# Attention loop of a transformer block: transposes moved in TensorE's order, scores in two PSUM banks

## What is computed

```python
q = (h @ Wq_c @ Wq_up).reshape(b, t, H, D).transpose(0, 2, 1, 3)         # 16 heads of 128
q = rmsnorm(apply_partial_rope(q, cos, sin), q_norm_w)
k_sw = rmsnorm(apply_partial_rope(h @ Wk, cos, sin), k_norm_w)
v_sw = h @ Wv
ck = rmsnorm(h.reshape(b, nb, M * HID) @ W_comp, k_norm_w)               # one key for 16 tokens
c_scores = jnp.einsum('bhtd,bnd->bhtn', q, ck) * scale
c_out = attend(c_scores, valid[None, None], sink, ck, 'bhtn,bnd->bhtd')
sw_scores = CAP * jnp.tanh(jnp.einsum('bhtd,bsd->bhts', q, k_sw) * scale / CAP)
sw_out = attend(sw_scores, sw_mask[None, None], sink, v_sw, 'bhts,bsd->bhtd')   # window of 128
ao = (c_out + sw_out).transpose(0, 2, 1, 3).reshape(b, t, G, H // G * D)
inter = jnp.einsum('btgf,gfi->btgi', ao, Wg)
return inter.reshape(b, t, G * INTER) @ Wo
```

## Time and profile before

| what | us |
|---|---|
| median of 3 runs | 987.6 |
| lowest, highest run | 986.24, 991.37 |
| the profiled execution | 990.28 |
| its span | 988.5 |
| PE busy in the span | 907.0 (92%) |
| DVE, ACT, POOL busy | 664.4, 570.2, 561.8 |

### The profile page before, as it was taken

The page is one execution under the profiler, slowest core; times in us unless marked ns, Lnnn a source line. Parts: engine busy times, 40 slices in busy tenths (PEclk is TensorE's granted clock), DMA queues, the critical chain, the costliest instruction groups (busy, mean ns, idle before and its releaser), DMA issues. The chain is left out here.

```text
span 988.5 us, 16804 instructions
## 1 busy us (share of the span) xinstructions
PE 907.0 (92%) x5022; PEld 771.4 (78%) x5022; DVE 664.4 (67%) x1256; ACT 570.2 (58%) x1565; POOL 561.8 (57%) x759
## 2 busy tenths in 40 slices
PE   4988898789999999999899999999859899999996
PEld 4987685578888888887788888888748688888885
DVE  4464559588888888889988888888846433332312
ACT  0544454577777777777777777777444523324221
POOL 0155100578898888888888889888323323222222
PEclk9998989999999999999999999999979999999999
DMA  8556667213224133141241331422071020020101
GB/s 284 186 203 235 212 217 227 89 43 126 68 71 146 43 117 111 52 144 48 78 140 55 119 96 51 152 87 82 12 266 75 1 85 1 1 86 1 43 0 44
DMA packets 68725, 101.29 MB, mean 102 GB/s; under 512 B 16176, under 2 KB 48432, under 8 KB 65712
## 3 DMA queue, kind: packets, MB, share of 16 engines
q1 hardware_dynamic: 56528, 72.65, 23.1%
q10 hardware_dynamic: 12128, 27.71, 7.8%
HBM read 82.64 MB, written 26.35 MB: 110 GB/s over the span
## 5 line engine op out<-in xcount | busy, mean ns | idle before, releaser
L1054 PE MATMUL banks<-fold,aoT 128*128 128x512 f32 x768 | 193.1, 400 | 0.0
L1854 POOL TENSOR_TENSOR gus<-arena,gus 128x512 fp32r<-128x512 f32 x43 | 64.8, 1507 | 183.2 <-ACT gus L1756 183.2
L1054 PEld LDWEIGHTS banks<-fold,aoT 128*128 128x128 f32 x768 | 139.5, 188 | 27.8
L1820 DVE SCALAR_TENSOR_TENSOR arena<-banks,sg,arena 128x512 f32<-128x512 f32 x44 | 33.0, 751 | 133.0 <-ACT arena L1751 133.0
L1054 PE MATMUL banks<-k_st,qT 128*128 128x256 f32 x768 | 106.9, 288 | 0.0
L1751 ACT ACTIVATE arena<-banks,sg 128x512 f32<-128x512 f32 x44 | 30.2, 687 | 124.7 <-PE banks L1710 124.7
L1710 PE MATMUL banks<-hT_even,w_hi 128*128 128x512 f32 x352 | 86.6, 398 | 12.5 <-issue 9.7
L1054 PEld LDWEIGHTS banks<-k_st,qT 128*128 128x128 f32 x768 | 95.3, 189 | 0.5 <-DVE qT L1323 0.5
L1674 PE MATMUL banks<-w_hi,gus 128*128 128x512 f32 x352 | 87.2, 390 | 1.9 <-DVE gus L1825 1.1
L1710 PEld LDWEIGHTS banks<-hT_even,w_hi 128*128 128x128 f32 x352 | 66.1, 191 | 27.9 <-issue 10.1
L1431 POOL TENSOR_TENSOR pp<-pp,kons 64x512 fp32r<-64x512 f32 x64 | 84.2, 1316 | 4.1 <-ACT pp L1194 4.1
(11 more groups left out here) (198 smaller groups left out, 2153.8 us busy)
## 6 DMA issues: line engine op xcount, KB each, us to landing
arena<-in_wq_blocks ACTq DMA_DIRECT2D x8, 1056.0 KB, 4.8
wq_words<-in_wq_blocks ACTq DMA_DIRECT2D x8, 1056.0 KB, 6.9
w_lo<-wq_words SPq DMA_DIRECT2D x11, 768.0 KB, 9.2
go_raw<-in_w_go SPq DMA_DIRECT2D x16, 512.0 KB, 6.8
k_st<-k_parts SPq DMA_DIRECT2D x32, 192.0 KB, 2.8
arena<-in_L_attn_h SPq DMA_DIRECT2D x32, 128.0 KB, 3.4
comp_raw<-in_w_comp SPq DMA_DIRECT2D x16, 256.0 KB, 4.0
v_st<-v_parts SPq DMA_DIRECT2D x32, 128.0 KB, 2.1
```

The lines of the kernel that those rows point to most:

```text
L1054: last = pe.matmul(out, lhs[a], rhs[b], start=start and q == 0 and u == 0, stop=stop and q == n - 1 and u == 2)
L1820: dve.scalar_tensor_tensor(gu[:, n % 2], GU[2 * (n % 2) + 1][:], sg[:, 1, h:h + 1], gu[:, n % 2], ALU.mult, ALU.mult).then_inc(gued, 1)
L1854: pool.tensor_tensor(gus[:, n % 2, 1], gu[:, n % 2], gus[:, n % 2, 0].bitcast(F32), ALU.subtract).then_inc(gu_lo, 1)
```

## The change

PE's order within a step is changed. The transposed queries stand directly behind the scores, and the compressed transposes stand between the two halves of the projection. The three kinds of transposes have a bank each: compressed in bank 2, probabilities in bank 3, queries in bank 5 as before. The scores of four heads, 256 columns each, go to banks 0 and 1, two heads in a bank. The waits on PE follow the banks. The leftover products use banks 2, 3, 6 and 7. On POOL `rotate` is written as two operations, one behind the other. The orders of ACT, DVE, POOL and SP stay. The diff, cut to its core (what is left out replaces `T` by `T_PROBS` or `T_COMP` in the evictions, and moves the helper `over` out of `rotate`):

```diff
--- before.py
+++ after.py
@@ -226,8 +226,8 @@
-UNIT_BANK = (0, 1, 6, 7)
-UNIT_FREE = (5, 6, 11, 12)
+UNIT_BANK = (2, 3, 6, 7)
+UNIT_FREE = (7, 8, 11, 12)
...
@@ -974,7 +974,8 @@
     Q, T, O, Y = bank[4:8]
-    S = banks[:, 0:4]
+    T_COMP, T_PROBS = bank[2:4]
+    S = banks[:, 0:2].rearrange("p b (u n) -> p (b u) n", n=KEYS)
...
@@ -1071,7 +1072,6 @@
         def transpose_query(g):
             wait(pe, "q_rope", g.n())
-            wait(pe, "cT_lo", g.n(2))
             wait(pe, "qT_lo", g.n(1))
...
             if opening(g, 0):
-                pe.wait_ge(units.f_lo, H - HG + 2)
+                pe.wait_ge(units.f_lo, HG + 2)
...
@@ -1097,21 +1097,20 @@
         def transpose_probs(g):
             wait(pe, "p_nrm", g.n())
             wait(pe, "p_nrm3", g.n())
+            wait(pe, "p_lo", g.n(1))
+            if opening(g, 0):
+                pe.wait_ge(units.f_lo, H - HG + 2)
+            for h in range(HG):
+                last = pe.transpose(T_PROBS[:, h * P:(h + 1) * P], prob[:, g.j, h, 0:P], ident)
+            last.then_inc(s["pT_mm"], 1)
+
+        def transpose_compressed(g):
+
+            wait(pe, "c_nrm", g.n())
             wait(pe, "cT_lo", g.n(1))
-            ahead = At(g.m, g.c + 1, 0)
-            if ahead.live:
-                wait(pe, "qT_lo", ahead.n())
-            for h in range(HG):
-                last = pe.transpose(T[:, h * P:(h + 1) * P], prob[:, g.j, h, 0:P], ident)
-            last.then_inc(s["pT_mm"], 1)
-
-        def transpose_compressed(g):
-
-            wait(pe, "c_nrm", g.n())
-            wait(pe, "p_lo", g.n())
             for pair in range(2):
                 cols = slice(pair * P, (pair + 1) * P)
-                last = pe.transpose(T[:, cols], pc[:, g.slot, cols], ident)
+                last = pe.transpose(T_COMP[:, cols], pc[:, g.slot, cols], ident)
             last.then_inc(s["cT_mm"], 1)
...
-        steps(pe, (0, query), (3, transpose_probs), (2, scores), (3, transpose_compressed), (4, project_first),
-              (4, project_second), (1, transpose_query), (3, window_values), (3, compressed_values), alone=EVERY,
+        steps(pe, (0, query), (3, transpose_probs), (2, scores), (1, transpose_query), (4, project_first),
+              (3, transpose_compressed), (4, project_second), (3, window_values), (3, compressed_values), alone=EVERY,
...
-            act.activation(pp[:, g.slot, HIGH], T[:], ACT.Copy).then_inc(s["p_hi"], 1)
+            act.activation(pp[:, g.slot, HIGH], T_PROBS[:], ACT.Copy).then_inc(s["p_hi"], 1)
...
         def rotate(g):
...
+        def rotate_rest(g):
+            x = qn[:, g.slot]
             wait(pool, "q_r1", g.n(1, 3) + 2)
...
         steps(pool, (3, masked_high), (0, square_sum), (0, rsqrt), (2, compressed_less_max), (5, add_tile),
-              (2, over_sum_last), (0, rotate), (2, compressed_over_sum), after={1: first_deviation})
+              (2, over_sum_last), (0, rotate), (0, rotate_rest), (2, compressed_over_sum), after={1: first_deviation})
```

More of the change, by code:

```diff
@@ L1110, in transpose_compressed @@
             wait(pe, "c_nrm", g.n())
-            wait(pe, "p_lo", g.n())
+            wait(pe, "cT_lo", g.n(1))
             for pair in range(2):
                 cols = slice(pair * P, (pair + 1) * P)
-                last = pe.transpose(T[:, cols], pc[:, g.slot, cols], ident)
+                last = pe.transpose(T_COMP[:, cols], pc[:, g.slot, cols], ident)
             last.then_inc(s["cT_mm"], 1)
@@ L1200, in compressed_high @@
                 rows = slice(half * NB, (half + 1) * NB)
-                last = act.activation(pcS[rows, g.slot, :, half], T[rows, 0:2 * P].rearrange("p (a n) -> p a n", n=P), ACT.Copy)
+                last = act.activation(pcS[rows, g.slot, :, half], T_COMP[rows, 0:2 * P].rearrange("p (a n) -> p a n", n=P), ACT.Copy)
             last.then_inc(s["cT_hi"], 1)
@@ L1303, in probs_low @@
             wait(dve, "p_hi", g.n())
[L1304 removed]
+            dve.tensor_tensor(pp[:, g.slot, LOW], T_PROBS[:], pp[:, g.slot, HIGH].bitcast(F32), ALU.subtract
                               ).then_inc(s["p_lo"], 1)
@@ L1310, in compressed_low @@
                 rows, across = slice(half * NB, (half + 1) * NB), slice((1 - half) * NB, (2 - half) * NB)
-                last = dve.tensor_tensor(pcS[across, g.slot, :, half], T[rows, 0:2 * P].rearrange("p (a n) -> p a n", n=P),
+                last = dve.tensor_tensor(pcS[across, g.slot, :, half], T_COMP[rows, 0:2 * P].rearrange("p (a n) -> p a n", n=P),
                                          pcS[rows, g.slot, :, half].bitcast(F32), ALU.subtract)
@@ L1449, in compressed_less_max, with over @@
                                ALU.subtract).then_inc(s["c_sub"], 1)
+        def over(g, lo, n):
+            return rope_st[:, g.tile_slot, lo:lo + n].unsqueeze(1).broadcast_to([P, HG, n])
         def rotate(g):
@@ L1454, in rotate @@
             wait(pool, f"rope_in{g.tile_slot}", g.loaded())
-            over = lambda lo, n: rope_st[:, g.tile_slot, lo:lo + n].unsqueeze(1).broadcast_to([P, HG, n])
             x = qn[:, g.slot]
-            pool.tensor_tensor(ropb[:, :, 0:HALF], x[:, :, HALF:2 * HALF], over(2 * HALF, HALF),
+            pool.tensor_tensor(ropb[:, :, 0:HALF], x[:, :, HALF:2 * HALF], over(g, 2 * HALF, HALF),
                                ALU.mult).then_inc(s["q_r1"], 1)
-            pool.tensor_tensor(ropb[:, :, HALF:], x[:, :, 0:HALF], over(3 * HALF, HALF), ALU.mult).then_inc(s["q_r1"], 1)
+            pool.tensor_tensor(ropb[:, :, HALF:], x[:, :, 0:HALF], over(g, 3 * HALF, HALF), ALU.mult).then_inc(s["q_r1"], 1)
+        def rotate_rest(g):
+            x = qn[:, g.slot]
             wait(pool, "q_r1", g.n(1, 3) + 2)
-            pool.tensor_tensor(x[:, :, 0:2 * HALF], x[:, :, 0:2 * HALF], over(0, 2 * HALF), ALU.mult).then_inc(s["q_r1"], 1)
+            pool.tensor_tensor(x[:, :, 0:2 * HALF], x[:, :, 0:2 * HALF], over(g, 0, 2 * HALF), ALU.mult).then_inc(s["q_r1"], 1)
             wait(pool, "q_r1", g.n(per=3))
```

1 line of the change is left out of this document (removed).

## The result

The changed kernel takes 1043.4 us (median of 4 runs, 1040.7 to 1049.0) against 986.9 for the kernel before (the 3 runs above and one more). The ratio is 1.057, with a 95% interval of 1.052 to 1.062: slower by 56.5 us. The forecast was 1046.4 us, 1030 to 1064, and slower with 0.92.

What follows compares the result with a forecast made beforehand. It took a loop over PE, ACT and DVE to bound the changed kernel: intervals of 60.4, 120.0 and 356.8 us made 537.2 against 480.4, +56.8, with the end +58.8, on the median of 987.6 giving 1046.4 us, range 1030 to 1064.

Steps and rivals of the forecast that it cites:

- The bound and the spare: Loop from query over compressed transposes, ACT and DVE to next query: 7.14 us before, under PE's 7.89, 0.75 to spare.
- the part on the banks: Shared score banks and separate transpose banks: gain nearly zero, since PE lost next to nothing there; at most 0.1 us a step.
- The ordinary steps: Forty intervals of the attention loop, set by the PE, ACT and DVE loop at 4.58 + 4.34 = 8.92 us each.
- The steps behind `add_tile`: Thirteen intervals with `add_tile` in POOL's row; the loop through POOL's rotation to the query transposes sets 9.23 us each.
- The steps at the start of a batch: Six intervals with two masking instructions between `compressed_max` and `window_sum` on DVE; 10.07 us each.
- the rival of the clock: PE's idling lowers its clock to 0.85 in the loop, adding 0.8 us in 59 intervals: 1094 us; chance 0.04.
- The end: After the last query: three steps about 1 us late each, against half a projection before PE's 3.19 us wait; +2 us, 0 to +4.
- The early query transposes: Query transposes behind the scores need `q_rope` early; ordinary loop through POOL 8.63 us, hidden under 8.92.
- ACT's own loop: From `compressed_high` through `over_sum` and PE back to the compressed transposes: 8.26 to 9.25 us, taken as 8.5, hidden under 8.92.
- PE as the bound: Rival: PE keeps 7.89 us a step and loses its 7.1 + 5.8 us of waits, about 975 us; chance 0.06.
- The loops of POOL and ACT alone: Rival: only these loops bind, ordinary steps 8.6 us, first of a batch 9.8, 1032 us in all; chance 0.12.
- The signs: Expected profile: steps about 8.9 us, PE idle 0.9 to 1.1 ahead of queries, ACT waiting at `compressed_high`, clock at 1.00.

Runs made afterwards that it cites:

- e9_add_tile_behind: The changed kernel with POOL's `add_tile` moved behind the rotation and `compressed_over_sum`; 1035.7 us, ratio 1.049 to the kernel before.
- e6_dve_only: The changed kernel with `compressed_low` moved behind `window_sum` and `scale_query` on DVE, ACT's order left; 1124.4 us, ratio 1.141 to the kernel before.
- e1_banks_only: The changed kernel with PE's order of before, keeping the new banks and waits; 981.9 us, ratio 0.995 to the kernel before.
- e3_compressed_late: The changed kernel with the query transposes back behind the projection, compressed transposes still between its halves; 1014.4 us, ratio 1.028 to the kernel before.
- e4_both_evictions_behind: The changed kernel with `compressed_high` behind tanh and exp on ACT, `compressed_low` behind `window_sum` and `scale_query` on DVE; 977.0 us, ratio 0.988 to the kernel before.
- e8_split_three: The changed kernel with three heads of the projection ahead of the compressed transposes and one behind, for two and two; 1101.7 us, ratio 1.118 to the kernel before.

## Why the prediction was right

**The bound and the spare.** The reasoning from the earlier trace rows held: from compressed transposes to query 4.34 us were read and 4.27 measured. One statement beside it was wrong: "nothing in it waits" did not hold for the step of the earlier trace rows: 0.25 us ahead of the compressed transposes were a wait, and PE's floor is 7.63 us. Without that wait the loop of the kernel before was 2.55 + 4.27 = 6.82 us, which is 0.81 under the floor, where I had 0.75. It changed no conclusion, but it is the term that was mis-sized. For the same reason the part on the banks was not quite right: "PE lost next to nothing there" leaves out these 0.25 us a step.

**The ordinary steps.** 8.92 us forecast, 8.74 measured, 40 of them: 7 us less. Query to compressed transposes is 0.77 + 0.35 + 1.51 + 0.35 + 1.48 = 4.46, not 4.58: the 1.51 stands against the 1.75 that held the wait, and in part made up for it are a longer query (0.77 for 0.69) and half projection (1.48 for 1.42). The way back is 4.27 for 4.34, most of it 0.41 for 0.47 from PE to ACT.

**The steps behind `add_tile`.** 9.23 forecast, 9.21 to 9.40 measured, 120.9 us in thirteen for 120.0; e9_add_tile_behind shows the cause.

**The steps at the start of a batch.** 10.07 forecast. Three of the six took 9.95 to 9.97 us, three 11.47 to 11.52. The difference is the clock. Two steps in a row and an ordinary one (stretch, length, busy us and instructions of PE, PEld, DVE, ACT and POOL, granted clock, DMA):

```profile
484.75:496.22 11.47, 9.03 (x46) 7.67 (x47) 8.40 (x18) 6.56 (x22) 7.97 (x12) 0.86 0.00 0
496.22:506.17 9.95, 7.54 (x46) 6.38 (x47) 8.32 (x17) 6.56 (x22) 7.00 (x11) 1.00 0.34 99
...
295.87:304.60 8.73, 7.88 (x49) 6.74 (x50) 7.13 (x15) 6.45 (x22) 6.82 (x11) 1.00 0.26 76
```

In the step from 484.75 the granted clock was 0.86 on average, that is, PE ran at the 1.2 GHz level for a part of it: its three query matmuls took 1.62 us for 0.93. PE had idled 2.42 us ahead of them. The next one had 2.44 us ahead of it and stayed at 1.00. Where the idle was 0.85 us a step, the clock stayed at 1.00 throughout. So the rival of the clock, to which I gave 0.04 for the whole loop, was true of three steps and cost 4.6 us. The Trainium skill (TensorE: Matmul & The Clock Gate, A second HAM failure mode: psum-queue depth-cycling) tells of a kernel in which short idles made the clock swing. The rows agree in part for idles of 2.0 to 2.5 us in a step of ten (three of seven here, about one in five in e6_dve_only), and do not for 0.85 us in 8.7.

The three parts give 349.7 + 120.9 + 64.4 = 535.0 us against the 537.2 of the sum: 7.1 us too much for the ordinary steps, 0.9 and 4.0 too little for the other two. That the sum was nearer than its terms is luck.

**The end.** +2 us estimated, 0 to 4; measured +4.8, outside of that. The lateness of the three steps came as forecast, 0.8, 1.0 and 1.0 us (728.01, 737.09, 746.04, 753.92 from step to step, for 682.01, 690.32, 698.29, 705.21 before). But I had set half a projection against PE's wait of 3.19 us. That wait only changed its name (PE, last query and the projection in that step):

```profile
728.01 0.93 PE L1055 MATMUL banks<-wup,q_st 128*128 128x512 f32 x3 [0.86 <-DVE qn L1331]
...
757.07 2.45 PE L1055 MATMUL banks<-fold,aoT 128*128 128x512 f32 x6 [2.50 <-DVE aoT L1277]
```

`project_first` needs `aoT`, whose low part stands on DVE behind the statistics for the next stage. PE waits 2.50 us for it, and the six matmuls then take 2.45 us instead of 1.64, at a granted clock of 0.62. The step that failed is that the wait "now has half a projection, 1.42 us, before it": DVE's queue held that half too.

**The other edits.** Banks: nothing forecast; in e1_banks_only the median is 5.7 us lower, the loop 1.8. The early query transposes: free, as said. ACT's own loop was hidden: PE waited for `over_sum` three times, all behind the last query.

**The rivals.** PE as the bound was out by 68 us. The loops of POOL and ACT alone, 8.6 us a step, would have come near the 8.74, but it is DVE's `qn` in front of the query that PE waits for in every ordinary step, and POOL's `qn` only 12 times; and with the query transposes late again (e3_compressed_late) half the loss stays. The Trainium skill (Perfetto Trace Analysis, Identifying the Most-Contended Engine) would have had the engine with the highest occupancy optimised first. By matmul busy time that was PE, the change took away waits of it, and the kernel became slower. The page also says to judge TensorE's headroom by MFU (the share of its peak arithmetic that is used) or by its weight loads; the loads were busy 54.59 us in the stretch of the earlier trace rows, just under POOL's 56.35, so that its rule did not clearly name PE here, nor does it give a time. e4_both_evictions_behind shows that PE's gaps could be closed, but by changing two other engines.

**The signs.** They held, but for sizes: PE idle 0.85 us, not 0.9 to 1.1, and the clock not at 1.00 in three steps.

## What to carry to other kernels

Before an instruction is moved back on the fullest engine, follow its result through the in-order queues of the others until it comes back, and compare the length of that loop with the step. An eviction that stands in front of unrelated work makes that work hang on it; moving the eviction back in the other queues can be what makes the move possible, and where two queues do it, both have to be changed. The slack of such a loop is read from steps in which each link is shown waiting for the one before; a step that shows no waits may still hold one.

## What the hardware showed that was not expected

The clock at idles of some 2 us: seven times in the loop of the changed kernel PE idled 2.0 to 2.5 us ahead of a query, and three of the steps that followed ran partly at the 1.2 GHz level (0.85 and 0.86 on average), four did not. In e6_dve_only it idled 2.0 us in each ordinary step of 9.9, and about one in five of them was hit. In e8_split_three it idled 1.42 us in each ordinary step of 9.43, and none of these was, only the first steps at and behind the start of a batch. What decides, these runs don't show.

DVE's 64x512 product of two tensors in SBUF (line 1317, now 1316) took 914 ns on average before and 1221 ns after, with no change to it. Its length goes with the time in which POOL's `masked_high`, a product of the same shape, runs beside it: 0.37 us of each before, 0.72 after, 0.10 in e4_both_evictions_behind (755 ns) and 0.02 in e6_dve_only (704 ns). No edit was made to test whether the one holds up the other, but the kept traces fit it.
